# Twelve of twenty TensorE transposes a batch become DMA transposes of bf16 parts, in a gated cross-attention kernel on one core

## The reference

```
x = x + tanh(g_xattn[0]) * L0_xattn(layernorm(x), ctx, ctx)       # first phase
x = x + tanh(g_ffn[0])   * L0_ffn(layernorm(x))                   # 8-bit-like rounding, one 256x256 product
x = x + tanh(g_xattn[1]) * L1_xattn(layernorm(x), ctx, ctx, mask) # 16 heads of 16
x = x + tanh(g_ffn[1])   * L1_ffn(layernorm(x))                   # 256 -> 1024, silu, 1024 -> 256

L1_xattn: query, key, value = q @ w_q.T + b_q, k @ w_k.T + b_k, v @ w_v.T + b_v, split into heads
          scores = query . key / sqrt(16), masked;  attn = softmax(scores);  out = (attn . value) @ w_o.T + b_o
L1_ffn:   h = layernorm(x) * gamma + beta;  z = silu(h @ w1 + b1) @ w2 + b2;  residual + 0.5 * z
```

## Time and profile before

| | |
|---|---|
| time of the kernel, median of 3 runs | 1608.69 us (1608.64 to 1610.67) |
| time of the profiled execution | 1610.62 us |
| its span, first to last instruction | 1608.8 us |
| TensorE busy | 1481.0 us, 92% |
| VectorE busy | 1317.8 us, 82% |
| ACT busy | 1134.1 us, 70% |
| GpSimd busy | 1033.2 us, 64% |
| mean granted TensorE clock | 0.961 |
| DMA queue of SP | 193520 packets, 124.46 MB, 26.5% of 16 engines |

### The profile page before, as it was taken

How to read it: one execution, slowest core, us unless ns; L and a number is a source line. 1 busy time by engine, 2 the same in 40 slices (tenths; PEclk the granted TensorE clock), 3 DMA queues, 4 the chain that set the end, 5 groups by cost and what they waited for, 6 DMA issues and landing times.

```text
span 1608.8 us, 42469 instructions
## 1 busy us (share of the span) xinstructions
PE 1481.0 (92%) x14155; PEld 1142.4 (71%) x14155; DVE 1317.8 (82%) x3187; ACT 1134.1 (70%) x2057; POOL 1033.2 (64%) x1392
## 2 busy tenths in 40 slices
PE   3899999999999972677999999999999999999997
PEld 2788888888888861434677777777777777777666
DVE  3798888888888875778888889898988889898742
ACT  7898888888888742355666666676666666676664
POOL 4688888888888744324556565666656565665445
PEclk8899999999999995588999999999999999999999
DMA  7322322322222002332223232323323232322200
GB/s 227 106 72 67 96 67 66 97 65 73 90 65 72 1 1 91 81 120 77 75 77 92 72 91 80 85 80 85 87 75 90 72 96 72 87 80 84 64 17 22
DMA packets 193593, 125.42 MB, mean 78 GB/s; under 512 B 40304, under 2 KB 192752, under 8 KB 193264
## 3 DMA queue, kind: packets, MB, share of 16 engines
q1 hardware_dynamic: 193520, 124.46, 26.5%
HBM read 92.69 MB, written 25.17 MB: 73 GB/s over the span
## 4 chain that ended last, share of the span: by engine, by line
PE 53%; DVE 3%; issue 2%; POOL 2%; ACT 1%; DMA 1%; SPq 0%; POOLq 0%
PE b_bank L1833 31%; PE b_bank L1908 7%; PE b_score L1873 5%; PE b_scoreT L1890 4%; PE b_bank L1841 3%; PE b_bank L1985 2%; DVE b_nm L1651 1%; PE b_bank L1923 1%; ACT b_E L1469 1%; DMA b_yT<-b_y 0%; POOL b_YT L1402 0%; PE b_scoreT L1858 0%; DVE b_xh L1740 0%; DVE b_v L1714 0%; POOL b_YT L1399 0%
## 5 line engine op out<-in xcount | busy, mean ns | idle before, releaser
L1469 ACT ACTIVATE b_E<-b_scoreT 128x1024 f32<-128x1024 f32 x256 | 262.0, 1023 | 149.9 <-PE b_scoreT L1890 148.9
L1651 DVE TENSOR_REDUCE b_nm<-b_score 128x4 bf16<-128x1024 f32 x256 | 313.3, 1224 | 52.2 <-PE b_score L1873 47.0
L31 ACT ACT_TABLE_LOAD x157 | 201.4, 1283 | 19.7 <-PEq L1059 16.4
L1833 PE MATMUL b_bank<-f,b_YT 128*128 128x256 bf16 x1536 | 191.4, 275 | 4.6 <-POOL b_YT L1402 4.6
L890 PE MATMUL bank<-hT,W1T 128*128 128x256 bf16 x1536 | 183.3, 273 | 2.6 <-DVE hT L706 1.9
L1833 PE MATMUL b_bank<-b_hT,f 128*128 128x256 bf16 x1536 | 183.4, 273 | 0.8 <-DVE X L1747 0.8
L890 PE MATMUL bank<-W2T,G 128*128 128x256 bf16 x1024 | 172.7, 274 | 6.6 <-DVE GT L780 6.1
L1833 PEld LDWEIGHTS b_bank<-f,b_YT 128*128 128x128 bf16 x1536 | 144.0, 99 | 40.3 <-issue 19.5
L1833 PEld LDWEIGHTS b_bank<-b_hT,f 128*128 128x128 bf16 x1536 | 147.7, 98 | 30.3 <-issue 12.6
L890 PEld LDWEIGHTS bank<-hT,W1T 128*128 128x128 bf16 x1536 | 148.0, 98 | 27.9 <-ACT G L549 4.0
L1386 POOL TENSOR_TENSOR b_v<-b_v,b_e 128x512 f32<-128x512 f32 x32 | 40.6, 1269 | 193.5 <-DVE b_e L1732 193.5
(11 more groups left out here) (222 smaller groups left out, 3516.7 us busy)
## 6 DMA issues: line engine op xcount, KB each, us to landing
b_Q<-q_dram SPq DMA_DIRECT2D x192, 64.0 KB, 2.6
b_K<-k_dram SPq DMA_DIRECT2D x192, 64.0 KB, 2.9
xin<-in_x SPq DMA_DIRECT2D x32, 256.0 KB, 3.1
ctxn<-in_ctx SPq DMA_DIRECT2D x32, 256.0 KB, 2.8
mask_in<-in_mask SPq DMA_DIRECT2D x32, 256.0 KB, 3.0
X<-in_x SPq DMA_DIRECT2D x32, 256.0 KB, 4.0
ctxt<-in_ctxT SPq DMA_DIRECT2D x32, 256.0 KB, 4.2
b_ctxt<-in_ctxT SPq DMA_DIRECT2D x32, 256.0 KB, 2.9
```

The costliest lines, as they stand in the source:

```text
L31: act.add_instruction(mybir.InstLoadActFuncSet(name=nc.get_next_instruction_name(), act_func_set_id=which, ins=[], outs=[]))
L1469: nc.scalar.activation(E[:, pair:pair + 2], scoreT_ps[:, :, :, :], ACT.Exp).then_inc(sig["E"], 1)
L1651: nc.vector.tensor_reduce(pair, score_ps[:, :, :, :], AX.X, ALU.max, negate=True).then_inc(sig["nm"], 1)
L1833: last = nc.tensor.matmul(out_tile, lhs(i, k), rhs(j, k), start=start and k == chunks[0] and (i, j) == TERMS[0], stop=stop and k == chunks ...
```

## The change

In the second phase the twelve TensorE transposes of xT, hT and oT are gone, with their three turns of PSUM banks. ACT now makes the bf16 part from the f32 tile in SBUF (xs, hs, os), VectorE subtracts it from that tile, both row-wise, and SP transposes both parts by one DMA of 128x1024 bf16 (256 KB) to xT, hT or oT. Their readers (`queries`, `hidden`, `output_projection`) wait for the landing of that DMA. xs is made one iteration earlier than its parts were: its part by ACT in the stage f, behind `silu(1)`. The context's parts cT have two buffers instead of one.

All orders are new. TensorE and SP are in the diff below. VectorE: normalised_low, maxima 0, attended 0 and 1, maxima 1, mlp_normalised, keys_low, maxima 2, attended_low, mlp_columns, scaled, maxima 3, mlp_low, quantised_update, maxima 4, queries_low, maxima 5, statistics_2, maxima 6, binades, attention_update, magic, mask_bias, result, maxima 7, attention_normalised, base. ACT: table of exp, keys_high, exponential 0, attended_high, exponential 1, mlp_high, exponential 2, queries_high, exponentials 3 and 4, heads_copy 0, exponentials 5 to 7, heads_copy 1, table of silu, silu 0 and 1, normalised_high, silu 2 and 3, values_copy. GpSimd: silu_parts 2 and 3 of w, mlp_bias, context_parts, output_bias, inverse_std_2, rounded, inverse_std_3, silu_parts 0 and 1 of h. The bank turns are: 6: F2, H2, V; 7: OT1, FFN, H1; 8: K, AV01, PROJ, H0; 9: OT0, Q, AV23, H3.

```diff
-        xT = sb("xT", [P, 2, C, S], BF16)
+        xs = sb("xs", [P, 2, T, D], BF16)
+        xT = sb("xT", [P, 2, T, C, P], BF16)
         ctxt = sb("ctxt", [P, C, S], F32)
-        cT = sb("cT", [P, 2, C, S], BF16)
+        cT = two("cT", [P, 2, C, S], BF16)
...
+                def transpose_parts(b, parts, columns, ready, freed, per, step):
+                    sp.wait_ge(sig[ready], done(b))
+                    sp.sem_inc(sig[step + "_parts"], 1)
+                    if (due := done(b, back=1, per=per)) is not None:
+                        sp.wait_ge(sig[freed], due)
+                    sp.sem_inc(sig[step + "_ready"], 1)
+                    sp.dma_start(columns[:, :, :, :, :].rearrange("p a t c s -> p (a t c) s"),
+                                 parts[:, :, :, :].rearrange("p a t d -> p (a t d)"),
+                                 transpose=True).then_inc(sig[f"{step}{b.parity}"], 16)
+
...
+                if q:
+                    transpose_parts(q, xs, xT, "xlo", "q_mm", 1, "xT")
+                if f:
+                    transpose_rounded()
+                if q:
+                    spill_keys()
                 if f:
                     load_context()
-                    transpose_rounded()
+                if o:
+                    transpose_parts(o, os, oT, "onlo", "proj_mm", 1, "oT")
                 if q:
                     spill_queries()
-                    spill_keys()
+                if h:
+                    transpose_parts(h, hs, hT, "hlo", "f1_mm", HC // 2, "hT")
+                if q:
+                    stack_keys()
                     stack_queries()
-                    stack_keys()
                 if m:
                     transpose_maxima()
+                    row_of_maxima()
                 if q:
                     load_mask()
-                if m:
-                    row_of_maxima()
                 if w:
...
                 def normalised_high():
-                    act.wait_ge(sig["xT_mm"], done(q))
-                    if (due := done(q, back=1)) is not None:
-                        act.wait_ge(sig["q_mm"], due)
-                    nc.scalar.activation(xT[:, 0], whole_bank(BANK["xT"]), ACT.Copy).then_inc(sig["xhi"], 1)
+                    act.wait_ge(sig["xh"], done(f))
+                    if (due := landed(f, back=1)) is not None:
+                        act.wait_ge(sig[f"xT{1 - f.parity}"], due)
+                    nc.scalar.activation(xs[:, 0], xh[:, :, :], ACT.Copy).then_inc(sig["xhi"], 1)
...
                 def normalised_low():
                     dve.wait_ge(sig["xhi"], done(q))
-                    nc.vector.tensor_tensor(xT[:, 1], whole_bank(BANK["xT"]), xT[:, 0], ALU.subtract).then_inc(sig["xlo"], 1)
+                    nc.vector.tensor_tensor(xs[:, 1], xh[:, :, :], xs[:, 0], ALU.subtract).then_inc(sig["xlo"], 1)
...
                 def queries():
                     free("Q")
-                    pe.wait_ge(sig["xlo"], done(q))
-                    column_projection("Q", 0, xT, "q_mm")
+                    pe.wait_ge(sig[f"xT{q.parity}"], landed(q))
+                    for c in range(C):
+                        last = product(by_rows(bank[BANK["Q"]][:, c]), lambda s, k: wqkvo[:, 0, s, k, tile(c)],
+                                       lambda s, k: xT[:, s, :, k, :], range(C))
+                    last.then_inc(sig["q_mm"], 1)
...
+                if m:
+                    scores(0)
                 if o:
                     heads_transposed(0)
-                if m:
-                    scores(0)
-                if o:
                     heads_transposed(1)
-                if q:
-                    normalised_transposed()
-                if h:
-                    mlp_transposed()
-                if w:
-                    second_product(0, 0)
-                if m:
-                    scores(1)
-                if a:
-                    scores_transposed(0)
-                if q:
-                    queries()
-                if m:
-                    scores(2)
-                if a:
-                    scores_transposed(1)
-                if o:
-                    attended_transposed()
                 if q:
                     keys()
                 if a:
+                    scores_transposed(0)
+                if m:
+                    scores(1)
+                if w:
+                    second_product(0, 0)
+                if a:
+                    scores_transposed(1)
+                if m:
+                    scores(2)
+                if q:
+                    queries()
+                if a:
                     scores_transposed(2)
-                if m:
-                    scores(3)
                 if w:
                     second_product(0, 1)
+                if m:
+                    scores(3)
+                if a:
+                    scores_transposed(3)
+                if w:
+                    second_product(1, 0)
                 if f:
                     quantised_product()
                 if a:
-                    scores_transposed(3)
                     values(0)
+                    scores_transposed(4)
                 if m:
                     scores(4)
                 if a:
-                    scores_transposed(4)
+                    values(1)
+                    scores_transposed(5)
+                if m:
+                    scores(5)
                 if o:
                     output_projection()
                 if a:
-                    scores_transposed(5)
-                    values(1)
-                if m:
-                    scores(5)
+                    scores_transposed(6)
+                if m:
+                    scores(6)
                 if a:
-                    scores_transposed(6)
+                    values(2)
+                    scores_transposed(7)
                 if w:
-                    second_product(1, 0)
+                    second_product(1, 1)
+                if m:
+                    scores(7)
+                if a:
+                    values(3)
                 if h:
                     hidden(0)
-                if a:
-                    scores_transposed(7)
-                if m:
-                    scores(6)
-                if w:
-                    second_product(1, 1)
-                if h:
                     hidden(1)
-                if m:
-                    scores(7)
-                if a:
-                    values(2)
-                    values(3)
-                if h:
                     hidden(2)
                     hidden(3)
                 if q:
...
```

More of the change, by code:

```diff
@@ L1560, in iteration @@
                     silu(1)
-                if a:
-                    heads_copy(1)
+                if f:
+                    normalised_high()
                 if h:
@@ L1836, in product @@
                 return last
-            def transposed(dst, src, step, by=ident):
-                for c in range(C):
-                    for t in range(T):
-                        last = nc.tensor.transpose(dst[:, c, t * P:(t + 1) * P], src[:, t, c * P:(c + 1) * P], by[:, :])
-                last.then_inc(sig[step], 1)
             def tile(t):
@@ L1972, in keys @@
                     pe.wait_ge(sig["ctlo"], done(q))
-                    column_projection("K", 1, cT, "k_mm")
+                    for c in range(C):
+                        last = product(bank[BANK["K"]][:, c], lambda s, k: wqkvo[:, 1, s, k, tile(c)],
+                                       lambda s, k: cT[q.parity][:, s, k], range(C))
+                    last.then_inc(sig["k_mm"], 1)
                 def values_in():
@@ L1986, in heads_transposed @@
                     last.then_inc(sig["oT_mm"], 1)
[L1988 to L1991 removed]
                 def output_projection():
                     free("PROJ")
[L1995 to L1999 removed]
+                    pe.wait_ge(sig[f"oT{o.parity}"], landed(o))
+                    for t in range(T):
+                        last = product(bank[BANK["PROJ"]][:, t], lambda s, k: oT[:, s, t, k, :],
+                                       lambda s, k: wqkvo[:, 3, s, k, :], range(C))
+                    last.then_inc(sig["proj_mm"], 1)
                 if m:
```

193 lines of the change are left out of this document (90 added, 103 removed).

## The result

The changed kernel takes 1625.39 us (median, 1624.39 to 1627.71), the kernel before, measured beside it, 1608.66 us: a ratio of 1.0103 (95% interval 1.0086 to 1.0121). It is 1.0% slower; the forecast was 1598 us. The profiled execution has a span of 1623.6 us, 14.8 us more than before.

A forecast was written before the change was run, and what follows sets the result against it. TensorE bounds the old kernel at 27.82 us a period; afterwards SP's queue loop, 27.4 us against the engines' 26.8, would set it. 26 periods save 11 us: 1610.6 to 1599.6, 1598 on the median's scale; range 1576 to 1624.

The forecast's parts named there:

- TensorE's own work: TensorE's pieces per period without the 12 f32 transposes: 26.5 us, 1.3 us saved.
- SP's queue: Deciding term: xT issued 11.95 us after the eighth transposed score, landing 3.6 us; loop closes at 27.4 us.
- Rival 3: DMA transposes' time grows with size: xT lands after 5.6 us, loop 29.4 us, 1650 us; chance 0.05.
- the line through two sizes: xT's landing extrapolated from transposes of two blocks (2.4 us) and four (2.8 us) to eight: 3.6 us.
- wait for oT or hT: At PROJ and H0: some 5 us of TensorE's other work cover a 3.6 us landing; cost nothing.
- The way back through TensorE: From Q to the next eighth transposed score: 11.6 us of TensorE work, 11.75 us with the wait at scores 5.
- the wait at scores 5: TensorE waits for maximum 4 behind the quantised update: 3.0 us against 2.86 us of work, about 0.15 us a period.
- with 0.2 us to spare: mlp_low ends at 5.4 us, the quantised product at 5.6, so quantised_update waits for TensorE, not VectorE.
- Rival 2: GpSimd's subtraction holds VectorE's mlp_low: scores 5 0.95 us later, SP's loop 28.35 us, 1622 us; chance 0.2.
- Rival 1: Engines alone set the period: xT lands in about 3 us, SP's loop under 26.8 us, 1582 us; chance 0.2.
- Ramp and tail: Iterations outside the steady stretch: some 8 us gain where TensorE bounds, +9 us in single-batch chains; nothing taken.
- The cover of V: Values 3 and H0 to H2 on TensorE cover xh; without them V starts late by up to 1.3 us.

The follow-up runs named there:

- e4: Changed kernel with rows of maxima last on SP, hn behind attended_low on VectorE, and GpSimd's output_bias behind inverse_std_2; 1603.33 us.
- e3: Changed kernel with SP's row_of_maxima behind mask load and store, VectorE's hn behind attended_low and ACT's mlp_high behind exponential 2; 1609.82 us.
- e1: Changed kernel with only SP's row_of_maxima moved behind the mask load and the store; 1630.47 us.
- e2: Changed kernel with VectorE's hn (mlp_normalised) moved behind attended_low and ACT's mlp_high behind exponential 2; 1620.70 us.
- e5: Changed kernel with only GpSimd's mlp_bias moved behind output_bias; 1627.30 us.
- e7: Changed kernel with less GpSimd work: fourth silu subtraction a one-input copy, mlp_bias on 16 of 256 columns, nothing moved; 1621.03 us.
- e12: e4 with less GpSimd work: context and fourth silu subtractions made one-input copies, mlp_bias on 16 of 256 columns; 1586.86 us.
- e6: e3 with VectorE's quantised_update moved behind maximum 5 and statistics_2 behind maximum 6; 1621.56 us.
- e8: Changed kernel with only VectorE's quantised_update moved behind maximum 5 and statistics_2 behind maximum 6; 1619.85 us.

## Why the prediction was wrong, point by point

**TensorE's own work: right in kind, mis-sized by 0.3 us.** 26.5 us were predicted, 26.78 are measured (26.73 in e4). The gain is 1.04 us a period and not 1.3. The chain of the changed kernel gives 6.66 us for five products run back to back where the sum had 6.55; the rest lies in pieces of a few hundredths.

**SP's queue: right, the landing in part by luck.** From the eighth transposed score at 954.82 to the issue of xT at 966.85 are 12.0 us, predicted 11.95; from there to queries at 970.55 3.70 us, predicted 3.6 and 0.1. Over the periods from 800 to 1500 us the two are 11.9 and 3.9 us on the average. The landings from 850 to 1500 us (median, the last number) show the size at work, and that xT, right behind the store, is the slowest of the three alike. First the changed kernel, then e3, where row_of_maxima stands between the store and xT:

```profile
b_xT<-b_xs SPq DMA_TRANSPOSE x23, 3.8
b_yT<-b_y SPq DMA_TRANSPOSE x23, 2.8
b_oT<-b_os SPq DMA_TRANSPOSE x23, 3.1
b_hT<-b_hs SPq DMA_TRANSPOSE x23, 3.1
b_nmT<-b_nm SPq DMA_TRANSPOSE x23, 2.4
```

```profile
b_xT<-b_xs SPq DMA_TRANSPOSE x24, 3.2
```

Rival 3 (time grows with size, 5.6 us) is out: 256 KB took 3.1 to 3.8 us. The 3.6 us of the line through two sizes came near xT's 3.8, but oT and hT of the same size took 3.1, and xT took 3.2 in e1, whose only change is SP's order, and in e3. So the order on the queue moves the landing by 0.6 us, which the line does not have. From the figure of the Trainium skill, Advanced Engine Details and Errata, section X-Bar Transpose (TRN2), 3.2 us had been estimated: that agrees with oT, hT and e3's xT, and is too short for xT of the changed kernel. No wait for oT or hT stands among TensorE's waits of the changed kernel; costing them at nothing was right.

**The way back through TensorE: this is the step that failed.** Its term for the wait at scores 5, 0.15 us a period, was 17.1 / 26 = 0.66 us. From queries at 970.55 to the next eighth transposed score at 983.25 are 12.70 us, predicted 11.75 (12.5 on the average of the periods from 800 to 1500 us). 0.73 us of the difference are scores 5, which waited 0.88 us and not 0.15; the rest is TensorE's own work, above. With 11.75 the loop would have closed at 27.5 us; it closes at 28.4 in this period. The wait at scores 5 lies in the loop that ends in xT, so VectorE's delay was paid in this loop even where TensorE seemed to wait for a DMA. The three runs that shorten hn bear this out. In e2, e5 and e7 scores 5 waits 0.50, 0.17 and 0.25 us a period less than in the changed kernel, queries wait for xT as long or longer (20.6 to 24.4 us in all), and the period is 0.22, 0.09 and 0.09 us shorter; with 1.5 us taken off for each fall of the clock (two, one and two, an estimate) 0.34, 0.14 and 0.20.

**Why scores 5 waited.** The prediction had quantised_update wait for TensorE, "with 0.2 us to spare". It doesn't: from 950 to 1500 us VectorE's line of that step has 0.3 us of idle time before it in 19 batches. It is VectorE that is late, by hn (1.99 us a batch, priced at 0.73) and by the update's own last step (1.05 us, priced as before, 0.75). In the period shown the update begins at 976.43, some 0.3 us behind the end of the quantised product (975.57 and 0.60), and takes 2.26 us to maximum 4, priced 1.57: there the update's own length is the larger part. mlp_low took 0.89 us, priced at 0.68. The price of a hold was in hand: the earlier trace rows has xh, of hn's shape, at 2.05 us beside a GpSimd subtraction. The prediction applied it to mlp_low alone and asked only where GpSimd's context parts would fall; it didn't ask the same of the silu parts, mlp_bias and output_bias, which the new order also sets beside other VectorE steps. e7 shows the cause for hn. For the update's last step it is e4: it fell from 948 ns in e3 to 752 when output_bias alone was moved away.

The Trainium skill, SBUF — State Buffer, section Who interferes with whom, counts tensor_scalar among the operations that can, depending on their operands, take the port pair shared with GpSimd, with one side blocked until the other's instruction is over. hn is a tensor_scalar, and its 0.73 us alone against 1.87 us here agree with that, though no run here shows the ports themselves; the prediction had quoted only the part on two inputs.

**The rivals.** Rival 2, slower by that hold, was right in mechanism: it had a loop of 28.35 us and 1622 us; measured are 28.30 us a period and 1625.39. That the size fits is luck. It put 1.16 us on mlp_low, which grew by 0.2; hn, which was left at 0.73, grew by 1.2 us a batch and the update by 0.3. It was given a chance of 0.2, because the rows didn't tell whether mlp_low would meet GpSimd, nor what two inputs in SBUF would do. Rival 1's time (1582 us, engines only) is what e12 comes near (1586.86), with SP's order mended and less work on GpSimd. SP's loop was not the only bound either: e1 took the wait for xT away, and scores 5 waited longer instead.

**Ramp and tail.** Nothing was taken, −8 to +9 us stated; measured are 2.3 us (−0.4 ahead of the stretch, +2.65 behind it).

**The cover of V.** The prediction said that values would start late, by up to 1.3 us, if TensorE's work no longer covered xh. In the changed kernel it does; in e6 and e8 it did not, at up to 0.7 us a period.

## What to carry to other kernels

Before a new order, set the two engines that hold each other side by side for a whole period, and price every step of one that falls beside a step of the other, not only those whose operands change; the price is in the old trace, at the place where they met before. A wait that is gone in one experiment while the time stays is not disproved as a cause: look at where the time went instead, here to the wait at scores 5 and to the clock (e1), and compare the kernel with both delays treated (e3). And where a step is held off the path, as xh was, leave it there: a hold that is moved falls on something else. It is no fixed sum: VectorE's same work was busy 23.7 us a period in e4 (616.22 / 26), 24.6 in the changed kernel and 25.0 in e6.

## What the runs showed of the hardware

VectorE's steps took up to two and a half times as long beside GpSimd: hn 0.73 and 1.87 us, v 0.73 and 1.84, the X update 0.75 and 1.32, os 0.68 and 1.20. GpSimd is stretched too: output_bias takes 1.86 us beside the X update, and took 1.41 us in the kernel before. A one-input GpSimd copy of 0.62 us held a VectorE subtraction as well (1.00 instead of 0.68 us).

In e1 TensorE's clock went to its lower level right behind a wait of 1.68 us, and the twelve matmuls that followed took 2.62 us; this came behind seven of nine waits of 1.66 to 1.80 us. In the changed kernel single waits of up to 1.8 us left the stretch at 1.00. What tells the two apart the runs here do not show.

One DMA transpose of 64 KB landed after 2.4 us, one of 128 KB after 2.8, one of 256 KB after 3.1 to 3.8 (medians), and each held SP's queue for 1.2 to 1.3 us of issue.
